# Query and key latents on GpSimd: four pieces of two row tiles in place of one block of eight

## The reference, cut to what matters

```python
q_lat = rmsnorm(hidden_states @ q_a_w, q_a_norm_w)                 # 192 columns
ckv = hidden_states @ kv_a_w
kv_lat, k_pe = (ckv[..., :KV_RANK], ckv[..., KV_RANK:])            # 64 and 64 columns
k_pe = rope_interleaved(k_pe[:, None, :, :], pos)
iq = (hidden_states @ idx_wq_w).reshape(b, s, IDX_H, IDX_D)        # 16 heads of 128
ik = hidden_states @ idx_wk_w
idx_scores = jnp.einsum('bqn,bnqk->bqk', iw, relu(jnp.einsum('bqnd,bkd->bnqk', iq, ik))) * IDX_D ** (-0.5)
_, topk_idx = jax.lax.top_k(idx_scores, TOPK)
gates = topv / jnp.sum(topv, axis=-1, keepdims=True)               # router: two best of eight experts
hw = h * w[:, :, None]
```

## Time and profile before

| | |
|---|---|
| median of three runs | 897.89 us |
| profiled execution, span from first to last instruction | 897.2 us |
| PE, DVE, ACT, POOL busy | 805.0, 675.8, 596.7, 531.0 us |
| index stage, first half | 44.5 to 114 us |
| index stage, second half, and last two row tiles | 114 to 282 us |
| attention | 282 to 880 us |
| TensorE's granted clock over the span | 0.985 |

### The profile page before, as it was taken

How to read it: one execution, slowest core, us unless ns; L and a number is a source line. 1 busy time by engine, 2 the same in 40 slices (tenths; PEclk the granted TensorE clock), 3 DMA queues, 4 the chain that set the end, 5 groups by cost and what they waited for, 6 DMA issues and landing times.

```text
span 897.2 us, 20231 instructions
## 1 busy us (share of the span) xinstructions
PE 805.0 (90%) x7496; PEld 500.7 (56%) x7496; DVE 675.8 (75%) x1557; ACT 596.7 (67%) x1340; POOL 531.0 (59%) x440
## 2 busy tenths in 40 slices
PE   4979989977777988898988899999999999999998
PEld 2445544444344655565555567777767777764443
DVE  5365677789998989999999788888888888861000
ACT  2656789978886878787887676776666767750000
POOL 3185368876884555545545587888878788840000
PEclk9989999999998999999999999999999999999999
DMA  8012211112333444443443288788778777880110
GB/s 254 24 36 74 80 41 54 58 31 85 105 114 89 130 125 115 131 111 111 136 129 105 65 137 167 135 137 155 149 147 147 141 137 152 165 168 15 68 51 32
DMA packets 168786, 96.67 MB, mean 108 GB/s; under 512 B 116720, under 2 KB 142704, under 8 KB 168688
## 3 DMA queue, kind: packets, MB, share of 16 engines
q1 hardware_dynamic: 168688, 95.37, 45.8%
HBM read 36.62 MB, written 6.29 MB: 48 GB/s over the span
## 4 chain that ended last, share of the span: by engine, by line
PE 28%; POOL 22%; DVE 21%; issue 15%; DMA 5%; SPq 4%; ACT 4%; POOLq 0%; DVEq 0%; ACTq 0%
PE psS L773 9%; DVE m L1176 5%; DMA arena<-arena 4%; DVE bias L1183 4%; DVE arena L1042 3%; DVE arena L1236 3%; SPq L451 3%; PE psS L700 3%; PE psT L572 2%; PE psT L552 2%; PE psS L529 2%; POOL arena L1356 2%; POOL arena L1469 2%; POOL bias L1422 2%; ACT arena L804 2%
## 5 line engine op out<-in xcount | busy, mean ns | idle before, releaser
L804 ACT ACTIVATE arena<-psT 128x512 f16<-128x512 f32 (+4 forms) x360 | 171.9, 506 | 107.0 <-PE psT L757 67.1
L700 PE MATMUL psS<-keyT,arena 128*128 128x512 f16 (+3 forms) x1152 | 232.6, 330 | 5.2 <-issue 3.0
L1236 DVE CUSTOM_DVE_ANT_0 arena<-psS,bias 128x512 f32<-128x512 f32 (+7 forms) x256 | 191.9, 751 | 36.7 <-PE psS L700 17.0
L991 ACT ACTIVATE arena<-arena,small 128x512 f32<-128x512 f32 (+7 forms) x256 | 197.5, 774 | 31.0 <-DVE small L1236 30.1
L1042 DVE SCALAR_TENSOR_TENSOR arena<-psT,arena 128x512 f16<-128x512 f32 (+3 forms) x278 | 146.1, 545 | 26.3 <-ACT arena L804 25.7
L757 PE MATMUL psT<-ident,arena 128*128 128x128 f32 x736 | 117.3, 281 | 26.3 <-DVE arena L1042 24.3
L700 PEld LDWEIGHTS psS<-keyT,arena 128*128 128x128 f16 x1152 | 92.6, 99 | 57.1 <-issue 8.1
L585 PE MATMUL psS<-ikT,big 128*128 128x512 f16 (+3 forms) x528 | 102.8, 339 | 23.9 <-DVE bias L1127 20.0
L757 PEld LDWEIGHTS psT<-ident,arena 128*128 128x128 f32 x736 | 86.1, 143 | 59.1 <-ACT arena L991 32.3
L1422 POOL TENSOR_TENSOR bias<-arena,bias 128x768 f32<-128x768 f32 (+2 forms) x48 | 91.4, 1918 | 32.7 <-ACT arena L870 22.3
L1183 DVE MATCH_REPLACE8 bias<-m,bias 128x768 f32<-128x768 f32 (+4 forms) x112 | 89.9, 809 | 0.0
(11 more groups left out here) (164 smaller groups left out, 1387.2 us busy)
## 6 DMA issues: line engine op xcount, KB each, us to landing
arena<-arena SPq DMA_DIRECT2D x192, 128.0 KB, 2.4
arena<-in_wiq SPq DMA_DIRECT2D x32, 256.0 KB, 2.7
arena<-in_ow SPq DMA_DIRECT2D x16, 512.0 KB, 3.5
arena<-in_qbT SPq DMA_DIRECT2D x16, 256.0 KB, 2.5
wvo_parts<-arena SPq DMA_DIRECT2D x16, 256.0 KB, 2.0
arena<-in_qpe SPq DMA_DIRECT2D x16, 128.0 KB, 3.0
arena<-in_x SPq DMA_DIRECT2D x8, 256.0 KB, 3.2
out<-arena SPq DMA_DIRECT2D x8, 256.0 KB, 2.0
```

The costliest lines, as they stand in the source:

```text
L700: last = mm(bank[:, k:k + w], Q[:, u % 2, h, a, q:q + P], keyT[:, b, h, k:k + w], start=(a, b) == (0, 0), stop=(a, b) == (1, 0))
L804: return nc.scalar.activation(dst, src, ACT.Copy, scale=scale)
L991: nc.scalar.activation(pr[:, g % 4, 0:kw], pr[:, g % 4, 0:kw], ACT.Exp, bias=shift[:, g % 4:g % 4 + 1], scale=-1.0, accum_out=rsum[:, unit ...
L1236: v.tensor_tensor_reduce(out=pr[:, g % 4, 0:kw], in0=bank[:, 0:kw], in1=bias[:, TOFF[t]:TOFF[t + 1]], scale=-c_s, scalar=3e38, op0=ALU.add ...
```

## The change

The query latents are made in four pieces of two row tiles each, `query_latents(0)`, `(2)`, `(4)` and `(6)`, with `wq_parts` of one head between pieces. The key's rotation is cut in two, `key_rope` (four products) and `key_turned` (subtracts and adds), again with one `wq_parts` between. The waits on `qn_done` count to 8 in place of 2, since each piece signals twice. Nothing else differs: the same numbers are computed.

```diff
-                src, ready, n = ((qn[:, :, 0:P], qn_done, 2), (qn[:, :, P:2 * P], qn_done, 2),
+                src, ready, n = ((qn[:, :, 0:P], qn_done, NT), (qn[:, :, P:2 * P], qn_done, NT),
...
-            def query_latents():
+            def query_latents(a):
+
+                two = slice(a, a + 2)
                 pool.wait_ge(rsn_done, 1)
-                link(mul(tmp, proj[:, :, C_Q:C_Q + QR], rsn[:, 0].unsqueeze(2).broadcast_to([P, NT, QR])))
-                mul(qn[:, :, 0:QR], tmp, qnw[:].unsqueeze(1).broadcast_to([P, NT, QR])).then_inc(qn_done, 1)
-                mul(qn[:, :, QR:256], tmp[:, :, P:QR], qnw[:, P:QR].unsqueeze(1).broadcast_to([P, NT, QR - P])).then_inc(qn_done, 1)
+                link(mul(tmp[:, two], proj[:, two, C_Q:C_Q + QR], rsn[:, 0, two].unsqueeze(2).broadcast_to([P, 2, QR])))
+                mul(qn[:, two, 0:QR], tmp[:, two], qnw[:].unsqueeze(1).broadcast_to([P, 2, QR])).then_inc(qn_done, 1)
+                mul(qn[:, two, QR:256], tmp[:, two, P:QR], qnw[:, P:QR].unsqueeze(1).broadcast_to([P, 2, QR - P])).then_inc(qn_done, 1)
...
-                pool.wait_ge(qn_done, 2)
+                pool.wait_ge(qn_done, NT)
...
+            def key_turned():
+                t4 = tmp[:, :, 0:128].rearrange("p t (f j) -> p t f j", f=4)
...
-            query_latents()
+            query_latents(0)
             wq_parts(3, 1)
+            query_latents(2)
+            wq_parts(4, 0)
+            query_latents(4)
+            wq_parts(5, 1)
+            query_latents(6)
+            wq_parts(6, 0)
             key_latents()
-            wq_parts(4, 0)
+            wq_parts(7, 1)
             key_rope()
-            wq_parts(5, 1)
+            wq_parts(8, 0)
+            key_turned()
+            wq_parts(9, 1)
             gated_rows()
-            for q in range(6, IH + 2):
+            for q in range(10, IH + 2):
                 wq_parts(q, q % 2)
```

## The result

| | before | changed |
|---|---|---|
| median of the first four runs | 897.97 us (897.49 to 898.2) | 892.74 us (892.44 to 895.81) |
| span of the profiled execution | 897.2 us | 891.2 us |
| mean granted clock in it | 0.985 | 0.992 |

The ratio is 0.9948, with a 95% interval of 0.993 to 0.9965: 5.2 us less. Two later series of twelve runs each, on two chips, gave 894.16 against 897.81 (ratio 0.9959, 0.9942 to 0.9976) and 894.87 against 898.99 (0.9966, 0.9947 to 0.9985), so 3.7 and 4.1 us less. Two executions of the kernel before in the second series (914 and 915 us) were in a slower state of the chip, and no figure here contains them. The forecast was 895.0, 2.9 us less.

What follows compares the result with a forecast made beforehand. GpSimd's order was taken to bound 53.5 to 73.1 us, 9.4 us lost. 3.4 us won less 0.5 us late gives 2.9; 897.2 less 2.9 is 894.3, plus 0.7 makes 895.0 us, range 892.3 to 896.9.

Steps and rivals of the forecast that it cites:

- The sum: 3.4 us won by query 6, less 0.5 us waiting ahead of query 10: 2.9 us won, 895.0 us.
- A piece of 2.25 us: GpSimd's time for one of four query-latent pieces: 0.82, 0.98 and 0.44 us of products plus 0.07 us of waiting.
- Weight parts 3 and 4 in time: GpSimd finishes these at 52.8 and 56.2 us, before TensorE wants them; the 4.58 us wait ahead of query 3 goes.
- VectorE's gates are late next: Head 3's scores wait for query 3's low part behind the router's gates, starting at 62.5 us; TensorE idles 3.6 us.
- How long the gates take: Five slow VectorE instructions wait for shorter GpSimd instructions, so the gates end at 61.9 us in place of 63.1.
- The half clock: Behind TensorE's standstill the clock stays at half for 4.53 us as before, costing 2.3 us.
- GpSimd's later parts: Blocks behind heads 7, 8 and 9 exceed the free 2.25 us, giving a 0.5 us wait ahead of query 10.
- The rest is shifted as it is: Behind 114 us the programs are the same and gated by semaphores, so everything there comes 2.9 us earlier.
- The 0.7 us around the span: The median before stood 0.7 us above the profiled span, so 0.7 is added to the forecast span of 894.3 us.
- Clock up: Rival: TensorE's clock stays up after the standstill, 2.3 us aren't lost, 5.2 us won, 892.7 us; chance 17%.
- Late gates: Rival: gates end only at 63.2 us and GpSimd is late before head 10, 0.4 us won, 897.5 us; chance 18%.
- Starved: Rival: blocked VectorE gates wait for one more short GpSimd instruction each, 0.7 us slower, 898.6 us; chance 7%.

Runs made afterwards that it cites:

- the four pieces without parts between: Changed kernel with all four query-latent pieces in a row ahead of head 3's weight part, rotation still split: 897.87 us, ratio 1.0004 to the kernel before.
- the filler: Changed kernel with 14 extra matmuls, results unused, in TensorE's standstill behind query 4: 893.51 us, ratio 0.9944 to the kernel before.
- the one-block rotation: Changed kernel with key_rope and key_turned in one block again between the weight parts of heads 7 and 8: 898.01 us, ratio 0.9999 to the kernel before.
- finer parts: Changed kernel with router's exponential and VectorE's gates moved early, rotation and gated rows cut in halves: 888.57 us, ratio 0.9893 to the kernel before.
- moving the gates: Router's exponential between ScalarE's ikT copies, VectorE's gates ahead of query 0's low part: 896.78 us on the kernel before, 890.00 on the changed one.

## Why the prediction was right, point by point

- **The sum.** 895.0 was forecast; the three series gave 892.7, 894.2 and 894.9. 2.9 us were forecast for the first half, 3.7, 3.4 and 3.4 were measured (42.22 less the three distances). The path was right: first weight part in time, VectorE's gates next, half clock behind the standstill, one late weight part. That the first series lay within the range is in part luck: 892.7 is 0.4 us from its lower end, and more than the path explains.
- **The first clue.** GpSimd's 22% of the chain of the whole span was taken as a sign that others wait for it here. It was no sign: the changed kernel shows 14, 22 and 17% in its three profiles. The busy times by stretch and the waits of TensorE carried the argument without it.
- **A piece of 2.25 us.** 49.98 to 52.26 in the profile after, 2.28. The single terms were 0.82, 0.98 and 0.44; measured 0.83, 1.00 and 0.46.
- **Weight parts 3 and 4 in time.** Right, queries 3 and 4 start 3.41 us apart with no wait.
- **VectorE's gates are late next.** Right. The scores of head 3 were forecast for 62.5 us and came at 62.80, which is 62.23 without the late start. The wait is 3.38 us, put down to L1042; 3.6 were forecast.
- **How long the gates take.** The end (61.9) was right within 0.2 us, the way to it only in part. The copy was to wait for the product forecast for 57.05 and slipped in ahead of it instead, and so did the compare; the product of L1150 then waited for the weight part. The margins were 0.02 to 0.03 us, which no sum from durations of 0.1 us can settle. In the third series' profile the copy slipped in too (0.18 us), but the compare waited for the weight part and the next two products for piece 4 (1.12, 0.78 and 0.98 us), as forecast, and the block took 5.6 us. So the end came within 0.2 us on two different ways, and on the first of them that is luck. The rule that the forecast drew from this pair was too simple: shorter neighbours alone don't mean shorter waits (6.9 us in the four pieces without parts between); the wait depends on which of them the instruction meets.
- **The half clock.** This is the term that was mis-sized: 2.3 us were taken over from the kernel before, and the profile after shows 1.7 (half of 3.4 us), the filler 1.6. The low stretch came when TensorE was at work again, and it was one stretch of 3.4 in place of one of 6.8.
- **GpSimd's later parts.** A wait of 0.5 us was forecast ahead of query 10. Query 10 starts 4.00 us behind query 9, 0.59 more than the pace. The sum behind it (2.25 us free between two parts, 1.9 of slack over all) also gave the 2.3 us of the one-block rotation and the end of the waits with finer parts.
- **The rest is shifted as it is.** From query 10 to query 16 that is so, 20.5 us in both profiles. Behind it the two profiles differ by 2.9 us more, with 10.2 us of half clock in place of 20.5. I had counted no chance for this, although had shown that the clock falls.
- **The 0.7 us around the span.** Wrong. The profiled execution after took 893.01 us with a span of 891.2, 1.8 more; the same 1.8 holds in each later run. So the profiled execution before took an estimated 899.0 us (897.2 + 1.8), 1.1 over its median: it was an execution with much half clock (27 us), and the difference of the two spans, 6.0 us, overstates the gain. In the sum the error cancels, since 897.2 and 0.7 together are just the median before.
- **The rivals.** Clock up: no, the clock fell; that its 892.7 is the first median to the tenth is chance. Late gates: no. Starved: no; a waiting VectorE instruction got in at the first boundary in all cases seen.

## What to carry to other kernels

When an engine does early what is wanted late, look at how much of it fits between two instructions that another engine waits for, head by head, and cut to that size: here 2.25 us of a 3.41 us pace, and with every block cut to that size and the gates out of the way no wait was left. Taking one bound away shows the next one, which may have cost nothing before: moving the gates was worth nothing measurable in the old order and 4 us in the new. To judge a change of 0.5%, compare the stretch it touches in several profiles, and neither the whole time nor the engines' shares of the chain over the whole span, as long as something random (here the clock) moves them as much.

## What the runs showed of the hardware that was not expected

- A 16-element copy on VectorE took 0.97 us beside a GpSimd product and 0.17 us when it started 0.03 us ahead of one. The Trainium skill (SBUF — State Buffer, "Who interferes with whom") says that the issue order decides which of the two waits; the trace agrees: the same instruction, two outcomes. The eight match-replaces (0.16 us) and the reciprocal (0.20 us) took the same beside a busy GpSimd and beside an idle one.
- Equal programs on one core differ from run to run by up to 6 us (892.16 to 898.53 in twelve runs of the changed kernel), and their time goes with the mean granted clock. A straight line through the 50 runs of the kernel before gives 0.25 us for each microsecond more at half clock, and leaves some 1 us of scatter.
